# Mixed attention: one score product behind the transposed scores, and the value product in halves of the queries

## What is computed

```python
q = (x @ wq.T + bq).reshape(b, h, t, d)      # b 4, h 16, t 512, d 8: a plain reshape, so a "head"
k = (x @ wk.T + bk).reshape(b, h, t, d)      # is a block of 32 tokens, and its 512 positions
v = (x @ wv.T + bv).reshape(b, h, t, d)      # run over these tokens and 16 groups of features
q, k = rope(q), rope(k)                      # one angle for all positions
p = softmax(q @ k.T / sqrt(d))
return (p @ v).transpose(0, 2, 1, 3).reshape(b, t, m) @ wo.T + bo
```

## Time and profile before

| | us |
|---|---|
| median of 3 runs (lowest, highest) | 5318.9 (5310.04, 5323.08) |
| the profiled execution | 5318.81 |
| its span, first to last instruction | 5317.0 |
| mixed attention from its first score product to its last output | 299.6 |

### The profile page before, as it was taken

The page is one execution under the profiler, slowest core; times in us unless marked ns, Lnnn a source line. Parts: engine busy times, 40 slices in busy tenths (PEclk is TensorE's granted clock), DMA queues, the critical chain, the costliest instruction groups (busy, mean ns, idle before and its releaser), DMA issues. The chain is left out here.

```text
span 5317.0 us, 123357 instructions
## 1 busy us (share of the span) xinstructions
PE 4797.5 (90%) x51848; PEld 3296.1 (62%) x51848; DVE 3247.7 (61%) x4325; ACT 2369.9 (45%) x2803; POOL 2772.0 (52%) x3572
## 2 busy tenths in 40 slices
PE   7799789999999999997688888789999999999996
PEld 3332356666666666664577777466666666666664
DVE  1365166666666666673566665366666666766663
ACT  2344145555555555553211111055555555555553
POOL 0000087777777777773111110187777777777772
PEclk9799889999999999998799998699999999999998
DMA  0000000000000000000000000100000000000000
GB/s 12 5 1 1 31 21 18 2 14 10 15 10 14 10 6 2 2 2 1 8 0 0 0 0 0 40 10 18 2 14 10 15 10 14 10 6 2 2 2 9
DMA packets 15066, 46.11 MB, mean 9 GB/s; under 512 B 4176, under 2 KB 6992, under 8 KB 12752
## 3 DMA queue, kind: packets, MB, share of 16 engines
q1 hardware_dynamic: 14544, 38.67, 2.1%
HBM read 37.61 MB, written 1.05 MB: 7 GB/s over the span
## 5 line engine op out<-in xcount | busy, mean ns | idle before, releaser
L718 POOL TENSOR_TENSOR w_qk<-w_turned 128x1024 f32<-128x1024 f32 x384 | 905.2, 2357 | 267.3 <-DVE w_turned L601 217.9
L596 DVE TENSOR_TENSOR w_turned<-w_ps_qk,w_rot_l 128x1024 f32<-128x1024 f32 x384 | 469.9, 1224 | 839.3 <-ACT w_squares L498 819.3
L305 PE MATMUL w_ps_y<-w_px,w_w_vo 128*128 128x128 f32 x6144 | 789.7, 284 | 116.3 <-ACT w_px L502 116.0
L305 PEld LDWEIGHTS w_ps_y<-w_px,w_w_vo 128*128 128x128 f32 x6144 | 754.0, 200 | 151.6 <-ACT w_px L502 130.3
L255 PE MATMUL w_ps_qk<-w_w_qk,ZT 128*128 128x512 f32 x1536 | 751.2, 612 | 37.3 <-DVE w_turned L601 17.2
L747 POOL TENSOR_TENSOR w_qk<-w_qk,w_inv_norm 128x1024 f32<-128x1024 f32 x384 | 723.3, 1906 | 0.0
L498 ACT ACTIVATE w_squares<-w_ps_qk 128x1024 f32<-128x1024 f32 x384 | 391.5, 1020 | 548.2 <-PE w_ps_qk L255 547.8
L601 DVE TENSOR_TENSOR w_turned<-w_ps_qk,w_rot_l 128x1024 f32<-128x1024 f32 x384 | 466.5, 1215 | 0.0
L605 DVE TENSOR_REDUCE w_sumsq<-w_squares 128x16 f32<-128x1024 f32 x384 | 455.3, 1186 | 0.0
L255 PEld LDWEIGHTS w_ps_qk<-w_w_qk,ZT 128*128 128x128 f32 x1536 | 266.5, 194 | 266.4 <-issue 242.1
L261 PE MATMUL w_ps_t<-ident,w_qk 128*128 128x128 f32 x3072 | 418.1, 280 | 5.4 <-ACT w_qT L531 5.4
(11 more groups left out here) (258 smaller groups left out, 9058.8 us busy)
## 6 DMA issues: line engine op xcount, KB each, us to landing
w_w_qk<-in_w_qk SPq DMA_DIRECT2D x12, 1024.0 KB, 4.9
w_w_vT<-in_w_vT SPq DMA_DIRECT2D x12, 512.0 KB, 3.5
w_w_o<-in_w_o SPq DMA_DIRECT2D x12, 512.0 KB, 5.2
w_w<-in_w SPq DMA_DIRECT2D x12, 384.0 KB, 3.0
w_w<-in_w SPq DMA_DIRECT2D x12, 192.0 KB, 3.1
XT<-in_x SPq DMA_DIRECT2D x1, 1024.0 KB, 4.8
w_rot<-in_rot SPq DMA_DIRECT2D x2, 512.0 KB, 6.1
out<-XT SPq DMA_DIRECT2D x1, 1024.0 KB, 4.8
```

The costliest lines, as they stand in the source:

```text
L305: last = nc.tensor.matmul(ps_y[:, D.t * P:(D.t + 1) * P].rearrange("p (a v q) -> p a v q", a=2, q=WIN), w_vo[:, D.parity, h, p, :], px[:, ...
L596: nc.vector.tensor_tensor(turned[:, which, 0, :].rearrange("p (h d) -> p h d", d=DH), flat(ps_qk[:]).rearrange("p (h d) -> p h d", d=DH), ...
L718: nc.gpsimd.tensor_tensor(qk[:, T.odd, which, :], turned[:, which, 0, :], turned[:, which, 1, :], ALU.add).then_inc(pool_add, 1)
```

## The change

In each step the second score product is issued behind the two transposed scores, no longer ahead of them. The value product of 128 keys is issued in two halves of 256 queries, the first in the step in which the whole one stood and the second in the step after it; `pe_o` counts when the second is issued. `pT` has six buffers, no longer four. The three last lags are one step longer, as the last value product of a unit ends a step later. The diff, without the lines that only move:

```diff
-ST_LAG, PV_LAG, TURN_LAG, ROWS_LAG, OUT_LAG = 10, 13, 21, 23, 25
+ST_LAG, PV_LAG, TURN_LAG, ROWS_LAG, OUT_LAG = 10, 13, 22, 24, 26
-        pT = sb("pT", [P, 4, 2, SEQ])
+        pT = sb("pT", [P, 6, 2, SEQ])
+            def scores(s, n, which):
+                if s >= PAIR_STEPS:
+                    return n
+                u, i = divmod(s, QPAIRS)
+                rows = pair_rows(i)[which]
+                if n >= RING:
+                    pe.wait_ge(dve_ring, n - RING + 1)
+                nc.tensor.matmul(ps[:, n % RING, :], block_of(QT, rows, u, i // 2), whole(KT, rows, u),
+                                 start=True, stop=True).then_inc(pe_ring, 1)
+                return n + 1
+
             n = 0
             for s in range(MIX_STEPS):
-                if s < PAIR_STEPS:
-                    u, i = divmod(s, QPAIRS)
-                    for rows in pair_rows(i):
...
-                        n += 1
+                n = scores(s, n, 0)
                 k = s - ST_LAG
...
                     last.then_inc(pe_st, 1)
+                n = scores(s, n, 1)
                 u, at = divmod(s - QPAIRS, QPAIRS)
...
-                m, at = divmod(s - PV_LAG, 2)
-                if at == 0 and 0 <= m < UNITS * KB:
+                m, half = divmod(s - PV_LAG, 2)
+                if 0 <= m < UNITS * KB:
                     u, a = divmod(m, KB)
-                    pe.wait_ge(act_e, 2 * m + 2)
-                    if a == 0 and u:
-                        pe.wait_ge(act_o, u)
+                    queries = slice(half * SEQ // 2, (half + 1) * SEQ // 2)
+                    if half == 0:
+                        pe.wait_ge(act_e, 2 * m + 2)
+                        if a == 0 and u:
+                            pe.wait_ge(act_o, u)
                     for r in range(QUADS):
                         k = 2 * m + (1 if r < 2 else 0)
-                        last = nc.tensor.matmul(ps[32 * r:32 * r + D0 + 1, O_BANK, :],
-                                                V[:, u // J0, QUADS * (u % J0) + r, a, :], pT[:, k % 4, r % 2, :],
-                                                start=a == 0, stop=a == KB - 1)
-                    last.then_inc(pe_o, 1)
+                        last = nc.tensor.matmul(ps[32 * r:32 * r + D0 + 1, O_BANK, queries],
+                                                V[:, u // J0, QUADS * (u % J0) + r, a, :], pT[:, k % 6, r % 2, queries],
+                                                start=a == 0 and half == 0, stop=a == KB - 1,
+                                                skip_group_check=True)
+                    if half == 1:
+                        last.then_inc(pe_o, 1)
...
-                    if k >= 4:
-                        act.wait_ge(pe_o, k // 2 - 1)
-                    nc.scalar.activation(pT[:, k % 4].rearrange("p a q -> p (a q)"),
+                    if k >= 6:
+                        act.wait_ge(pe_o, k // 2 - 2)
+                    nc.scalar.activation(pT[:, k % 6].rearrange("p a q -> p (a q)"),
```

## The result

The changed kernel took 5284.4 us (median of 4, 5280.6 to 5291.0) against 5315.5 (4 runs), ratio 0.9942, interval 0.9925 to 0.9959: about 31 us faster, where 22 were forecast. The sign and the mechanism of the score loop came as predicted; the time lies 3.6 us under the range (5288 to 5316). Two more measurements of the same kernel gave 0.9945 (0.9930 to 0.9960) and 0.9939 (0.9926 to 0.9952). Over all runs the changed kernel has a median of 5284.4 (16 runs) and the kernel before 5313.8 (67 runs), each spread by some 6 us (standard deviation). The kernel before differed between the sets of runs: its medians were 5315.5, 5314.7, 5310.8 and 5316.5. Beside the first, the second and the fourth the changed kernel ran too, and was 31.1, 31.1 and 31.0 us faster.

A forecast was written before the change was run, and what follows sets the result against it. The loop through the score ring was taken to bound the mixed attention, not TensorE's work: -24.4 us in the steady part plus 2.8 in the tail made -21.6, from 5318.8 to 5297 us; range 5288 to 5316.

The forecast's parts named there:

- The ring's loop: Mixed attention: first score product, maximum, then next step's second score product; 1.91 us, 3.52 a pair of steps after change.
- many times shorter each: Waits of score weight loads for VectorE's maxima, 65.4 us in 98 waits before, would stay but each be many times shorter.
- The partner between the passes: Second score product of a step, issued last, would start between the other three products' passes, on average 0.15 us late.
- Rival 3: Second score product, once late, waits for the others' second passes, 0.53 us behind; pair 4.28 us, kernel 5341; chance 0.05.
- The half product: Value product of 256 queries on TensorE: 0.55 us each, bounds 0.49 to 0.98, against 0.98 for the whole.
- rivals 1 and 4: Halves cost 0.63 to 0.85 us each, 5308, chance 0.13; or 0.98 like a whole, 5335, 0.07 with other slower ends.
- The copy of `oT`: ScalarE's copy behind its step's exponential ends before the next unit's first half, some 0.15 us to spare; costed at nothing.
- rival 2: The `oT` copy comes late, 0.3 us in each of 16 units; 4.8 us of the gain go, 5302; chance 0.08.
- The pair and the steady part: Two steps of mixed attention fall from 3.945 to 3.52 us; over 57.5 pairs, steps 13 to 127, 24.4 us saved.
- the escape from the queue: Transposed score products no longer queue behind the ring's wait and start beside the first score product; nothing added or taken away.
- The tail: Steps 128 on, without scores: 16.8 us becomes 19.6, so 2.8 us lost.
- The start: Steps 0 to 12 of the score loop, at the low clock: zero, with 3.4 us either way.

## Why the prediction was right and where it was wrong

- **The bound.** Right. The ring's loop set the pace before and after; shortening the maximum shortened the cycle until TensorE's own work took over. The waits of the score loads did not become "many times shorter each": 0.42 us against 0.67, and fewer than half as many.
- **The partner between the passes.** Right: 0.02 to 0.31 late in the steady steps, 0.15 on average, as forecast. Rival 3 is out: the partner, last of the four products in the program, starts its first pass 0.33 ahead of the others' second ones (420.07, 420.40). The Trainium skill ("TensorE: Matmul & The Clock Gate", section "The mechanism") says that matmuls start strictly in program order. These rows do not agree, for passes of products in different quarters of the array. For them "strictly in the order written", as the kernel was described, holds for products and not for their passes.
- **The half product.** 0.56 for 0.55; rivals 1 and 4 are out. **The copy of `oT`:** no wait for it appears in the steady part; rival 2 is out.
- **The pair and the steady part.** 3.50 for 3.52 (steps of 1.86 and 1.64), 25.4 us saved for 24.4.
- **The split of the causes.** The prediction gave the order no gain of its own, only the escape from the queue. Measured: 20 us of the stage from the halves, 4 from the order on top (3.5 by itself).
- **The tail.** Forecast 2.8 lost. Counted from the last score product, the last value pass comes 2.1 later, the next stage 1.9 to 2.9.
- **The start.** Costed at nothing; it gave 1.5, 1.7 and 2.5 in three profiles. The transposed scores of steps 10 to 12, at the low clock, start beside the first score product, and this comes with the order (2.5 with the order alone, nothing with the halves alone). The granted clock rose earlier too: 26.2, 25.9 and 23.6 us into the loop in these profiles and 23.3 with the order alone, against 29.8 to 30.5 in the kernel before. Why it rose earlier stays open.
- **The sum, the step that failed.** It set the saving of the stage against 5318.8, one execution of the kernel before, and put the start and the rest of the kernel at nothing. Of the 12.6 us between 5297.0 and 5284.4, 3.3 are the base: the median beside the changed kernel was 5315.5. Another 3.3 are the stage: it saved 24.2, 24.4 and 26.2 us (24.9 on average) where 21.6 were forecast, with 1.0 more than forecast in the steady part, 1.5 to 2.5 at the start and up to 0.9 in the tail. The last 6 are outside the score loop, and no run explains them. Against the median of all 67 runs (5313.8) the base would be 5.0 and this remainder 4.3, but 17 of those runs are from a set in which the changed kernel did not run. The standard error of the difference of the two kernels is about 1.7 us (6.0 and 5.9 spread over 16 and 67 runs), without what differs from set to set. The stretch ahead of the loop, 1.9 us shorter on average in the three profiles, moves between executions of one kernel. Whether a real gain of a few microseconds hides there stays open.
- **The range** had the price of every edit in it, and nothing for the rest of the kernel, whose executions alone spread by 6 us. Its lower end was 3.6 us too high.

## What to carry to other kernels

When an engine is "busy" throughout and another waits for it in turn, write the loop through the ring buffer as a sum of durations; then ask what work stands inside that loop between the late instruction and the next start, and spread it evenly: here cutting one block of 0.98 us in two was worth twenty microseconds of the stage, and moving what stood behind the wait was worth four. Check such a theory by shortening the member of the loop that has idle time.

Before summing against one execution, see where it lies among the runs, and give the untouched stages their own share of the range.

## What the runs showed of the hardware

- At the start of the score loop of the kernel before, TensorE was busy for 28.8 of 29.6 us at a granted clock of 0.50. With a product of all 128 rows in each of the first ten steps it was busy without a gap from 215 to 245 us, and the clock stayed at 0.50 too. There it rose 37.2 us into the loop, 2 us ahead of the first transposed score product; in the 13 other profiles it rose 2 to 10 us behind it. So the transposed scores alone do not explain when it rises.
- The 128 one-column products ahead of the loop, spread over four column quarters and some 14 ns a matmul, stall for 1.3 to 2.3 us 256 instructions apart, where a block of code is fetched. The 256 added behind the attention, all in one quarter and at most 54 ns apart, met no stall; they cost 24.9 us.
- Stages with the same instructions took 1864.5 to 1875.7 us (first windowed layers) and 850.5 to 856.9 us (delta memory) in six profiles.
